# Causal mask of the attention row maxima: a matmul ahead of the scores instead of a mask operand on VectorE

## What is computed

```python
scores = jnp.einsum('bhqd,bhkd->bhqk', q, k) / jnp.sqrt(jnp.asarray(dk, x.dtype))
causal = jnp.tril(jnp.ones((S, S), dtype=bool))
scores = jnp.where(causal, scores, jnp.asarray(-jnp.inf, x.dtype))
probs = jax.nn.softmax(scores, axis=-1)
attn = jnp.einsum('bhqk,bhkd->bhqd', probs, v)
```

## Time and profile before

| What | Value |
|---|---|
| median of three runs | 569.86 us |
| the profiled execution's own time | 569.19 us |
| its span in the profile | 567.3 us |
| PE (TensorE matmul) busy | 461.5 us, 81% of the span |
| DVE (VectorE) busy | 400.5 us, 71% |
| ACT (ScalarE) busy | 285.7 us, 50% |
| POOL (GpSimd) busy | 280.3 us, 49% |
| mean granted TensorE clock | 0.925 of 2.4 GHz |

### The profile page before, as it was taken

How to read it: one execution, slowest core, us unless ns; L and a number is a source line. 1 busy time by engine, 2 the same in 40 slices (tenths; PEclk the granted TensorE clock), 3 DMA queues, 4 the chain that set the end, 5 groups by cost and what they waited for, 6 DMA issues and landing times.

```text
span 567.3 us, 10534 instructions
## 1 busy us (share of the span) xinstructions
PE 461.5 (81%) x3243; PEld 284.8 (50%) x3243; DVE 400.5 (71%) x1308; ACT 285.7 (50%) x531; POOL 280.3 (49%) x403
## 2 busy tenths in 40 slices
PE   3687778888898999799968989999998469679860
PEld 3645456666653444334323445344455138579760
DVE  4689738999654888688987888889994235434741
ACT  1568696654453443536335776687866342112230
POOL 4210028999400786668431385675925502644742
PEclk9879799999799999999977999999998878969995
DMA  8800000000002332566800042234440120132112
GB/s 354 207 1 1 0 1 2 0 2 0 9 0 91 116 96 57 157 158 183 176 15 3 4 112 71 79 92 136 128 145 3 39 71 16 44 99 72 47 52 75
DMA packets 28350, 41.35 MB, mean 73 GB/s; under 512 B 3548, under 2 KB 19868, under 8 KB 27388
## 3 DMA queue, kind: packets, MB, share of 16 engines
q1 hardware_dynamic: 24136, 31.33, 19.2%
q0 software_dynamic: 4160, 9.35, 5.6%
HBM read 27.98 MB, written 12.48 MB: 71 GB/s over the span
## 4 chain that ended last, share of the span: by engine, by line
PE 46%; DVE 19%; issue 11%; POOL 8%; ACT 7%; DMA 5%; SPq 1%; another core or an unknown queue 1%; DVEq 1%; POOLq 0%; ACTq 0%
PE ps L1882 5%; PE ps L1987 4%; PE ps L1996 3%; PE ps L1818 3%; DVE arena L1284 3%; PE ps L1820 3%; PE ps L1755 3%; PE ps L1766 2%; PE ps L1868 2%; PE ps L1593 2%; PE ps L1790 2%; DVE st L440 2%; POOL qk_parts L347 2%; PE ps L1681 2%; DMA arena<-expert_weights 1%
## 5 line engine op out<-in xcount | busy, mean ns | idle before, releaser
L1284 DVE CUSTOM_DVE_ANT_0 arena<-ps,const 128x512 bf16<-128x512 f32 (+3 forms) x256 | 110.8, 486 | 7.8 <-PE ps L1790 7.4
L844 ACT ACTIVATE arena<-ps 128x256 f32<-128x256 f32 (+3 forms) x128 | 85.0, 703 | 46.2 <-PE ps L1868 39.4
L557 POOL TENSOR_TENSOR arena<-arena 128x512 f32<-128x512 f32 x32 | 45.7, 1428 | 59.5 <-DVE arena L1253 59.4
L1790 PE MATMUL ps<-arena 48*128 48x128 bf16 (+3 forms) x256 | 51.4, 310 | 9.8 <-DVE arena L1284 6.0
L1882 PE MATMUL ps<-arena 128*32 128x512 f32 (+3 forms) x512 | 51.8, 470 | 1.3 <-issue 1.3
L913 ACT ACTIVATE arena<-ps 128x512 f32<-128x512 f32 x30 | 17.9, 597 | 63.9 <-PE ps L1987 31.9
L1868 PE MATMUL ps<-arena 51*128 51x128 bf16 (+3 forms) x256 | 49.9, 314 | 0.0
L1863 PE MATMUL ps<-bconst 64*128 64x64 bf16 x512 | 43.3, 195 | 7.2 <-ACT arena L844 6.0
L1987 PE MATMUL ps<-arena 128*128 128x128 f32 x240 | 36.4, 300 | 13.2 <-DVE arena L1461 8.2
L656 POOL DMA_INDIRECT tokens_y<-arena,token_at x30 | 29.0, 965 | 35.8 <-DVE arena L1474 31.4
L1790 PEld LDWEIGHTS ps<-arena 48*128 48x128 bf16 x256 | 17.3, 95 | 53.7 <-DVE arena L1284 30.0
(11 more groups left out here) (249 smaller groups left out, 1102.4 us busy)
## 6 DMA issues: line engine op xcount, KB each, us to landing
arena<-expert_weights SPq DMA_DIRECT2D x32, 256.0 KB, 4.0
arena<-moe_in SPq DMA_DIRECT2D x4, 1025.0 KB, 4.9
qk_parts<-arena SPq DMA_DIRECT2D x24, 128.0 KB, 3.0
qk_parts<-arena POOLq DMA_DIRECT2D x24, 128.0 KB, 2.5
arena<-qk_parts POOLq DMA_DIRECT2D x32, 96.0 KB, 2.5
slots_x<-zeros SPq DMA_DIRECT2D x1, 1980.0 KB, 21.0
arena<-slots_x SPq DMA_DIRECT2D x6, 330.0 KB, 3.9
moe<-moe_in SPq DMA_DIRECT2D x1, 1936.0 KB, 13.6
```

The source lines that it names most:

```text
L557: pool.tensor_tensor(yacc[:, ts], yacc[:, ts], pr[:, i % 2, :], ALU.add).then_inc(sem("yacc"), 1)
L844: act.activation(pt[:, u % 4, :, 0:n], ps[:, 4 + 2 * k:6 + 2 * k, 0:n], ACT.Exp, scale=ATT_SCALE).then_inc(sem("probs"), 1)
L1284: v.tensor_tensor_reduce(out=junk[:, done % 2, 0:n], in0=ps[:, k, col:col + n], in1=w["mask"][:, (3 - qt) * P:4 * P], scale=1.0, scalar=3 ...
L1790: mm = pe.matmul(ps[:, k, col:col + n], qaug[lo:lo + KR, b % 2, 2 * g + j // 2, qt * P:(qt + 1) * P], kaug[lo:lo + KR, b % 2, 2 * g + j // ...
```

## The change

The mask leaves VectorE. Ahead of each unit TensorE now multiplies a constant bf16 matrix `future` (128 x 128: a large negative number where the key lies after the query) with the identity, into the last 128 columns of each head's scores; this matmul has all 128 rows and starts the bank, and the scores are added to it. VectorE then takes the maximum with a plain `tensor_reduce`. A unit now holds parts of one `qt` alone, one or two heads, and one instruction takes the maxima of both heads (`qt` 0 and 1). The 16 parts make 12 units: `FIRST_PASS` is dealt anew, one unit in each of slots 0, 1, 2 and 4, two in each of slots 3, 5, 6 and 7. Counts of the semaphore `mx` go from 16 to 12 for a group, the scratch tile goes, and the constant `mask` (512 float32 columns) is no longer loaded; `future` is 128 bf16 columns.

```diff
--- before.py
+++ after.py
@@ -53,9 +53,9 @@
     "attn": [("wq", 128), ("wqs", 128), ("wk", 128), ("wks", 128), ("wv", 128), ("wo", 128)],
     "moe1": [("wr", 8), ("W1", 4096), ("W2", 4096)],
     "const": [("ident", 128), ("tri", 128), ("after", 128), ("cos", 512), ("sin", 512), ("iota", 8),
-              ("mask", 512), ("segment", PT * E1), ("full", PT), ("block", NBLK), ("number", NT), ("spare", PARTS * NBLK)],
+              ("segment", PT * E1), ("full", PT), ("block", NBLK), ("number", NT), ("spare", PARTS * NBLK)],
 }
-BPACK = [("identb", 128), ("causal", 256), ("half", 64)]
+BPACK = [("identb", 128), ("causal", 256), ("half", 64), ("future", 128)]
 
 
 def offsets(fields):
@@ -201,7 +201,6 @@
         wog = used.take(B * D).rearrange("p (b d) -> p b d", b=B)
         ropet = ar.take(4 * S).rearrange("p (k t) -> p k t", k=4)
         qk = ar.take(2 * S).rearrange("p (k t) -> p k t", k=2)
-        junk = ar.take(2 * S, BF16).rearrange("p (k t) -> p k t", k=2)
         assert ar.at <= VA
         xb = [arena[:, later + 2048 * a:later + 2048 * a + NBLK * ROW].rearrange("p (j d) -> p j d", d=ROW)
               for a in range(PARTS)]
@@ -246,21 +245,21 @@
         FIRST_PASS = [
             [[(3, 0)]],
             [[(3, 1)]],
-            [[(2, 0), (0, 0)]],
-            [[(2, 1), (0, 1)]],
             [[(1, 0), (1, 2)]],
+            [[(0, 0), (0, 2)], [(0, 1), (0, 3)]],
             [[(1, 1), (1, 3)]],
-            [[(3, 2)], [(3, 3)]],
-            [[(2, 2), (0, 2)], [(2, 3), (0, 3)]],
+            [[(3, 2)], [(2, 0)]],
+            [[(3, 3)], [(2, 1)]],
+            [[(2, 2)], [(2, 3)]],
         ]
+        MAXIMA = 12
         ring = []
 
-        units, at_slot, maxima_done = [], [], [0]
+        units, at_slot = [], []
         for slot in FIRST_PASS:
             at_slot.append(range(len(units), len(units) + len(slot)))
             for parts in slot:
                 units.append(parts)
-                maxima_done.append(maxima_done[-1] + len(parts))
 
         ROPE_AT = {(2, 0): 0, (2, 1): 1, (2, 2): 2, (2, 3): 2, (3, 0): 4, (3, 1): 5, (3, 2): 6, (3, 3): 6}
 
@@ -288,13 +287,13 @@
                     ring_projection(n, j)
             if r >= DENSE - 8:
                 for u in at_slot[r - DENSE + 8]:
-                    ring.append((("mx", 0, u), ("mx", maxima_done[u + 1])))
+                    ring.append((("mx", 0, u), ("mx", u + 1)))
         RING_PREPARED = len(ring)
         for it in range(-1, 16):
             for i in range(8):
                 if it + 2 < 16:
                     for n in at_slot[i]:
-                        ring.append((("mx", it + 2, n), ("mx", 16 * (it + 2) + maxima_done[n + 1])))
+                        ring.append((("mx", it + 2, n), ("mx", MAXIMA * (it + 2) + n + 1)))
                 if i == 3 and 0 <= it + 1 < 16:
                     ring.append((("mT", it + 1), ("mT", it + 2)))
                 if i == 3 and 0 <= it - 1:
@@ -571,7 +570,7 @@
             def max_parts(s):
 
                 k = s % 2
-                pool.wait_ge(sem("mx"), 16 * (s + 1))
+                pool.wait_ge(sem("mx"), MAXIMA * (s + 1))
                 pool.tensor_copy(mpc[:, k, :, :, 0], mx[:, k]).then_inc(sem("m_parts"), 1)
                 pool.wait_ge(sem("m_parts"), 4 * s + 1)
                 pool.tensor_tensor(mres[:, :, :], mx[:, k], mpc[:, k, :, :, 0], ALU.subtract).then_inc(sem("m_parts"), 1)
@@ -1275,17 +1274,11 @@
                 k = ring_read(v, "mx", s, u)
                 if u == 0 and s >= 2:
                     v.wait_ge(sem("m_parts"), 4 * (s - 1))
-                col = 0
-                for c, (qt, j) in enumerate(units[u]):
-                    n = P * (qt + 1)
-                    done = 16 * s + maxima_done[u] + c
-                    if done >= 2:
-                        v.wait_ge(sem("mx"), done - 1)
-                    v.tensor_tensor_reduce(out=junk[:, done % 2, 0:n], in0=ps[:, k, col:col + n],
-                                           in1=w["mask"][:, (3 - qt) * P:4 * P], scale=1.0, scalar=3 * NEG,
-                                           op0=ALU.add, op1=ALU.max, accum_out=mx[:, s % 2, qt, j:j + 1])\
-                        .then_inc(sem("mx"), 1)
-                    col += n
+                qt, j = units[u][0]
+                heads_in, n = len(units[u]), P * (qt + 1)
+                v.tensor_reduce(mx[:, s % 2, qt, j:j + 2 * heads_in - 1:2].unsqueeze(2),
+                                ps[:, k, 0:heads_in * n].rearrange("p (h n) -> p h n", h=heads_in), AX_X, ALU.max)\
+                    .then_inc(sem("mx"), 1)
 
             weigh(0)
             for i in range(33):
@@ -1783,14 +1776,16 @@
                 elif b == 0 and g == 1 and i == 0:
                     pe.wait_ge(sem("aug0"), 192)
                 k = ring_bank("mx", s, i)
-                col = 0
-                for qt, j in units[i]:
-                    n = P * (qt + 1)
+                heads_in, n = len(units[i]), P * (units[i][0][0] + 1)
+                pe.matmul(ps[:, k, 0:heads_in * n].rearrange("p (h n) -> p h n", h=heads_in)[:, :, n - P:n], w["future"],
+                          identb.unsqueeze(1).to_broadcast([P, heads_in, P]), start=True, stop=True,
+                          skip_group_check=True)
+                for c, (qt, j) in enumerate(units[i]):
                     lo = HALF * (j % 2)
-                    mm = pe.matmul(ps[:, k, col:col + n],
+                    mm = pe.matmul(ps[:, k, c * n:(c + 1) * n],
                                    qaug[lo:lo + KR, b % 2, 2 * g + j // 2, qt * P:(qt + 1) * P],
-                                   kaug[lo:lo + KR, b % 2, 2 * g + j // 2, 0:n], start=True, stop=True)
-                    col += n
+                                   kaug[lo:lo + KR, b % 2, 2 * g + j // 2, 0:n], start=False, stop=True,
+                                   skip_group_check=True)
                 mm.then_inc(sem("ring_ps"), 1)
 
             def y0_T(n):
@@ -2045,11 +2040,9 @@
     d = np.arange(P) % DK
     cos = np.cos(ang)[:, d // 2].T
     sin = np.sin(ang)[:, d // 2].T * np.where(d % 2 == 0, -1.0, 1.0)[:, None]
-    mask = np.zeros((P, 4 * P), np.float32)
-    mask[:, 3 * P:4 * P] = np.where(k[None, :] > k[:, None], NEG, 0.0)
     const = {
         "ident": np.eye(P), "tri": k[:, None] <= k[None, :], "after": k[:, None] > k[None, :],
-        "cos": cos, "sin": sin, "iota": np.broadcast_to(8.0 - np.arange(8), (P, 8)), "mask": mask,
+        "cos": cos, "sin": sin, "iota": np.broadcast_to(8.0 - np.arange(8), (P, 8)),
         "segment": np.broadcast_to(np.arange(PT * E1) % PT > 0, (P, PT * E1)),
         "full": np.broadcast_to(P * np.arange(PT), (P, PT)),
         "block": np.broadcast_to(np.arange(NBLK), (P, NBLK)),
@@ -2061,6 +2054,7 @@
         "causal": np.concatenate([np.where(k[None, :] > k[:, None] % HALF + HALF * qh, NEG, 0.0) for qh in range(2)],
                                  axis=1),
         "half": k[:, None] % HALF == np.arange(HALF)[None, :],
+        "future": np.where(k[:, None] > k[None, :], NEG, 0.0),
     }
     fc = np.concatenate([np.asarray(const[n], np.float32) for n, _ in PACKS["const"]], axis=1)
     bc = np.concatenate([np.asarray(bconst[n], np.float32) for n, _ in BPACK], axis=1).astype(np.dtype("bfloat16"))
```

## The result

| | before | after |
|---|---|---|
| median of four runs each, side by side | 570.82 us (569.84 to 573.41) | 610.79 us (605.09 to 612.29) |
| the profiled execution | 569.19 us | 612.29 us |
| PE busy | 461.5 us, 81% | 519.0 us, 85% |
| DVE busy | 400.5 us, 71% | 393.4 us, 64% |
| mean granted TensorE clock | 0.925 | 0.902 |

The ratio is 1.067 (95% interval 1.059 to 1.076): slower by 40 us. Forecast were 614 and a range of 588 to 632. The profiled execution of after is the slowest of its four; the fastest, 605.09 us, had a mean clock of 0.915.

A forecast was written before the change was run, and what follows sets the result against it. PE was taken as the bound, DVE close behind. Per group 0.85 + 1.71 + 1.07 - 0.7 = 2.9 us; 14 groups 41, plus 1.5, 0.5 and 1.5, gave 44.5 us more: 614 us, range 588 to 632.

The forecast's parts named there:

- lost overlap: TensorE scores: masks between slots cut the halves' side-by-side work, 2560 columns, 1.07 us a group (bounds 0 to 1.4).
- waits that vanish: PE's waits for DVE end as DVE gets less work: 0.7 us taken off each group.
- rival A: DVE is the bound, masks fall into PE's waits, each group gains 0.4 us: 564 us, chance 0.05.
- rival C: PE fills the gaps, no tile change or overlap lost: 0.15 us a group, 572 us, chance 0.05.
- Mask columns: TensorE: 12 mask matmuls a group, 2048 columns hidden by nothing, 0.85 us a group.
- Changes of tile: TensorE: 19 more array-shape changes a group around the masks, 0.09 us each, 1.71 us.
- rival B: Tile changes are free for bf16: a group costs 1.2 us more, 588 us, chance 0.12.
- rival E: The masks' weight loads are exposed: 1.1 us more a group, 629 us, chance 0.10.
- The clock in iteration 0: Iteration 0 runs partly at 1.2 GHz, where its 4608 columns cost more: 1.5 us.
- Rival D: More matmuls from 289 to 305 us may keep the clock at 2.4 GHz: 609 us, chance 0.10.
- Groups 0 and 1 and the rest: Early groups: 1.5 us for group 0, 0.5 for group 1; rest of the kernel 0.
- the two-headed pattern: DVE maxima over two heads: same distances as one head assumed, 0.4 us less a group; might eat all savings.

The follow-up runs named there:

- E7: Kernel before with plain tensor_reduce in place of the fused tensor_tensor_reduce, mask left out, its own 10 units kept: 568.9 us, ratio 0.997.
- E3: Changed kernel with each mask matmul cut to 8 of its 128 columns a head, number and places kept: 595.6 us, ratio 1.045.
- E8: Changed kernel plus 17 unread whole-array matmuls of 512 columns ahead of masks of groups 1 and 2: 599.4 us, ratio 1.049.
- E9: Kernel before plus 14 unread whole-array matmuls of 448 columns ahead of units of groups 1 and 2: 574.5 us, ratio 1.011.
- E6: Changed kernel without mask matmuls, its 12 units dealt anew so both array halves get the same columns: 576.0 us, ratio 1.008.
- E10: Kernel before, its own 10 units, with plain maxima and two 64-row mask matmuls in the array half ahead of each part: 575.9 us, ratio 1.010.
- E2: Changed kernel with the mask made by two 64-row, 64-column matmuls a head in the half its scores use: 580.9 us, ratio 1.025.
- E4: Changed kernel with both masks first, then both units' scores, in slots 3, 5, 6 and 7: 596.8 us, ratio 1.048.

## Why the prediction was right

The forecast was 3 us from the median, and its mechanism holds, but three of its terms (the lost overlap, the waits that vanish, the clock) were off and cancel in part; so near a hit is luck.

- **What bounds the kernel.** Right. PE had 0.7 us of slack in the iteration that was read and 1.3 in others (below), and took every added matmul on itself; rival A (DVE as the bound) and rival C (gaps filled) needed waits that weren't there. E7 adds little to this, since plain maxima are hardly cheaper: 0.60 us from start to start for 512 columns where it was 0.61.
- **Mask columns**, 0.85 us a group. Right: E3 takes 1920 of the 2048 away and gains 0.80.
- **Changes of tile**, 19 of 0.09 us. Right in the steady iterations (9 to 28 changes, 0.09 to 0.11 each), so rival B (free for bf16) falls. Whether the 0.1 us is the change itself, or a weight load (95 to 98 ns) that can't run ahead across a change, no run here tells apart; a load on top of the change, rival E, isn't there.
- **Lost overlap**, 1.07 us. Mis-sized: too large by 0.4. The time in which a matmul of either half streams, from starts and columns, is 3.07 us of the iteration of the earlier trace rows and 3.73 of the same one after: 0.66 more. In before it would be 2.56 if the halves ran side by side as fully as the prediction's columns have it. The sum of the iteration closes: columns 0.85, changes 2.0 (the 28 add up to 2.85, the 9 to 0.86), overlap 0.66, less 0.64 of waits (below), is 2.87 of 2.88.
- **The waits that vanish**, 0.7 us a group. Right in the iteration that I had read, too small elsewhere. From the distances of PE's starts, less columns and changes of tile, PE stood for 0.70 us in the iteration of the earlier trace rows, and for 0.06 after. In groups 4 to 11, where projections of other sequences lie between, it stood for 10.5 us in eight iterations and for 2.2 after: 1.05 less in each. Those projections also have the mask's shape and save changes, 17.4 instead of 19. The prediction had checked its 0.7 against the idle time between PE's records, 0.6 an iteration; records outlast their columns, so that short stands don't show there. So these steps grew by 2.1 us by GpSimd's marks, 2.3 by VectorE's last maxima (GpSimd came 1 us late to group 11 before), not 2.9. Groups 4 to 15 grew by 29.0 instead of 34.8: 9.8 of columns, 21.8 of changes and 7.9 of overlap, less 10.4 of waits, where the prediction's terms make 10.2, 20.5, 12.8 and 8.4 before rounding. This is the term "14 x 2.9" of the sum.
- **The clock in iteration 0**, 1.5 us. In proportion this is the step that was most off, the other way. I had taken the stretch at 1.2 GHz as of fixed length, with its added columns at double price. It grew from 13.7 to 34.1 us and took in the whole of iteration 1: group 3's step grew by 8.0 where 2.9 was forecast, and E8 gives 11.4 us of the median back by removing the stretch. Rival D had the clock stay up because PE's gaps fill. In the stretch they did fill, and it stayed down; the wait of 0.68 us right ahead of it was left. The Trainium skill, "TensorE: Matmul & The Clock Gate", Part 1, has activity release the clock; E8 agrees with that. Two stretches here don't: PE is busy for 33.49 of 33.90 us at 0.50 in after, and for 23.70 of 23.70 in E9.
- **Groups 0 and 1 and the rest**: 1.7 and 1.2 us measured, 1.5 and 0.5 forecast; the tail took 1.2 us that I had at 0.
- **DVE**: the two-headed pattern costs no more than one head of the same columns, as taken. What the prediction didn't see is the deal's own price: the 12 units cost 7 us in a kernel where PE still waits for banks (E6 against E7). I had expected no such waits; in after they are indeed short, since the masks fill them.

By the profiled execution the forecast was 34.8 for groups 4 to 15, 7.3 for groups 2 and 3 with the clock, 2.0 for groups 0 and 1, 44.5 in all as rounded there; 29.0, 10.0, 2.9 and a tail of 1.2 came, 43.1. The total is closer than its terms.

## What to carry to other kernels

Moving work from a busy engine to another helps only if the other one has idle time in the same stretch: read this from the starts in one iteration, and from several iterations, not one. On TensorE a small matmul is priced by what stands on either side of it: here its own columns were about a third of its cost, and the same mask in the shape of its neighbours cost about a fifth of the whole-array one (7 us in E10, 6 in E2, against 35). Work that an engine does inside a pass that it makes anyway, like the mask operand here, is the first thing to leave where it is.

## What the runs showed that I had not expected

- TensorE stayed at 1.2 GHz for 33.9 us while PE was busy for 33.49 of them. 17 whole-array matmuls of 512 columns removed the stretch in one kernel, and with it the wait that stands ahead of it everywhere else; 14 of 448 in the other left that wait (1.40 us), and the stretch there was longer with them (23.7 against 13.7 us).
- A maximum over two heads of 256 columns takes 686 ns, to the nanosecond the time of one head of 512, and as long as the fused addition and maximum of 512 columns (0.69 us) that it replaces.
- Putting two masks side by side (E4) saves two changes of tile and then loses 0.36 us of it in slot 7, because the second mask asks for its bank before VectorE has let it go.
